# Relational layer of a graph network: loop product and bias made in the table stage, output stage written out

## The reference

```
W = (w_comp @ w_basis).reshape(8, 128, 128)      # one matrix per node type, from 4 bases
decomp(h) = einsum('ni,tio->tno', h, W)[node_type, arange(n)]
k, q, v = decomp_k(x), decomp_q(x), decomp_v(x)
kt = einsum('nhi,thij->tnhj', k, relation_att)[edge_type, src]     # vt likewise from v
e  = (q[dst] * kt).sum(-1) * relation_pri[edge_type] / 4
a  = softmax of e over the edges of each dst
agg = segment_sum(a * vt, dst)                   # sums divided by the softmax's sum
out = relu(decomp_a(agg) + x @ loop_weight + bias)
x = layernorm(x + out)
```

## Time and profile before

| | |
|---|---|
| median of 3 runs | 13184.11 us (13170.3 to 13192.89) |
| the profiled execution's own time | 13179.73 us |
| its span | 13177.8 us |
| PE, DVE, ACT, POOL busy | 52%, 50%, 16%, 53% of the span |
| mean granted clock of PE | 0.635 |

### The profile page before, as it was taken

How to read it: one execution, slowest core, us unless ns; L and a number is a source line. 1 busy time by engine, 2 the same in 40 slices (tenths; PEclk the granted TensorE clock), 3 DMA queues, 4 the chain that set the end, 5 groups by cost and what they waited for, 6 DMA issues and landing times. The chain is left out here.

```text
span 13177.8 us, 169349 instructions
## 1 busy us (share of the span) xinstructions
PE 6872.9 (52%) x37679; PEld 6012.4 (46%) x37680; DVE 6549.5 (50%) x22663; ACT 2082.2 (16%) x6208; POOL 7027.7 (53%) x7417
## 2 busy tenths in 40 slices
PE   5555444445554555100384555656666566665555
PEld 4444333335554555100234455456665465654444
DVE  6444455555555555200265555755556344455555
ACT  4222100001110111000121111311222111122222
POOL 6555566646664666777205555245553555535554
PEclk6555555556666666555687777877787555556766
DMA  0000011111111111010143222111112211112232
GB/s 19 1 1 1 21 44 44 44 42 42 42 43 40 42 42 43 16 22 8 50 157 79 74 74 74 56 38 39 39 39 65 52 38 38 38 47 77 79 81 74
DMA packets 436083, 614.60 MB, mean 47 GB/s; under 512 B 176625, under 2 KB 312133, under 8 KB 435173
## 3 DMA queue, kind: packets, MB, share of 16 engines
q0 software_dynamic: 257024, 486.93, 14.5%
q1 hardware_dynamic: 178369, 119.49, 3.2%
q10 hardware_dynamic: 292, 3.41, 0.1%
HBM read 520.17 MB, written 89.19 MB: 46 GB/s over the span
## 5 line engine op out<-in xcount | busy, mean ns | idle before, releaser
L1094 POOL DMA_INDIRECT hop_rows<-hops,k_src_gather x1568 | 1479.3, 943 | 1077.3 <-issue 435.9
L1137 PE MATMUL hop_sums<-hop_rows,hop_weighted 128*128 x4992 | 1159.9, 405 | 1110.7 <-DVE k_x L1184 736.1
L1137 PEld LDWEIGHTS hop_sums<-hop_rows,hop_weighted 128*128 128x128 f32 x4992 | 1009.7, 300 | 1201.7 <-issue 1200.4
L1443 POOL DMA_INDIRECT l_pass_rows<-related,k_dst_typed x832 | 786.2, 945 | 1216.8 <-POOLq L74 517.6
L1443 POOL DMA_INDIRECT l_pass_rows<-left_table,k_dst_other x832 | 786.6, 945 | 895.7 <-DVE l_pass_terms L1815 490.5
L1938 POOL DMA_INDIRECT l_weigh_rows<-row_table,l_weigh_ring x832 | 813.0, 977 | 733.8 <-ACT l_weigh_ring L1902 466.3
L1443 POOL DMA_INDIRECT l_pass_rows<-key_table,k_src_gather x784 | 739.5, 943 | 766.6 <-DVE l_pass_scores L1752 387.3
L726 POOL DMA_INDIRECT src_sorted<-src_scatter_records,src_scatter_places x784 | 750.6, 957 | 606.3 <-DVE src_scatter_places L714 393.6
L1538 PE MATMUL l_pass_sums<-l_pass_zero 128*128 128x272 bf16 (+1 forms) x1210 | 262.7, 306 | 1454.0 <-DVE l_total L1632 1005.2
L1094 POOL DMA_INDIRECT hop_rows<-in_x,k_src_gather x784 | 739.6, 943 | 456.4 <-issue 220.8
L1292 POOL DMA_INDIRECT dst_sorted<-rec,dst_places x784 | 809.2, 1032 | 262.1 <-issue 262.1
(11 more groups left out here) (467 smaller groups left out, 18342.8 us busy)
## 6 DMA issues: line engine op xcount, KB each, us to landing
related<-l_tables_rows SPq DMA_DIRECT2D x50, 1024.0 KB, 4.4
hop_rows<-hops,k_src_gather POOLq DMA_INDIRECT x1568
l_pass_rows<-related,k_dst_typed POOLq DMA_INDIRECT x832
l_pass_rows<-left_table,k_dst_other POOLq DMA_INDIRECT x832
l_weigh_rows<-row_table,l_weigh_ring POOLq DMA_INDIRECT x832
src_sorted<-src_scatter_records,src_scatter_places POOLq DMA_INDIRECT x784
hop_rows<-in_x,k_src_gather POOLq DMA_INDIRECT x784
dst_sorted<-rec,dst_places POOLq DMA_INDIRECT x784
```

Of the source, the lines that this page charges most:

```text
L1094: nc.gpsimd.indirect_dma_start(rows[:, s * G + g, :], None, table_in, bass.IndirectOffsetOnAxis(ap=o.gather[:, c:c + 1], axis=0),).then_in ...
L1137: last = nc.tensor.matmul(sums[:, b, g, :], weighted[:, s % SLOTS, g, :], rows[:, bass.ds(slots[g], 1), :], start=True, stop=True)
L1443: nc.gpsimd.indirect_dma_start(rows[:, s, g, :], None, table, bass.IndirectOffsetOnAxis(ap=index[:, c:c + 1], axis=0),).then_inc(got[s], 16)
```

## The change

In `relation_tables`, each step also makes `x @ loop_weight + bias` of its block: a 1-row product of ones with the bias and a 128x128 product accumulate in `turned[:, 1, :]`, ACT copies them to `looped`, and SP stores the block (64 KB) in `looped_home` in HBM. `relation_output` loads that array in five pieces instead of computing it, has no bias, no `inputs`, no `by`: POOL multiplies the sums by the inverses, PE turns them where they stand in `total`, the products have three buffers instead of two, DVE reads the type weights in `mix` and starts its chain from `looped`. The stage is written out for 25 pairs and has no loop. Removed lines of `relation_output` are left out below; they stand in the listing above.

```diff
-def relation_tables(nc, k, bases, att_sb, msg_sb, mix, queries, table, name, shared=None):
+def relation_tables(nc, k, bases, att_sb, msg_sb, mix, queries, table, loop_w, bias, looped_home, name, shared=None):
...
+            sp.dma_start(wl[:], loop_w).then_inc(loaded, 16)
+            sp.dma_start(bias_row[:], bias.rearrange("(a f) -> a f", a=1)).then_inc(loaded, 16)
             with sp.Fori(0, NBD // 2) as i:
                 for b in range(2):
                     n = i * 2 + b
+                    sp.wait_ge(looped_ok, n + 1)
+                    sp.dma_start(looped_home[:, bass.ds(n, 1), :], looped[:, b:b + 1, :]).then_inc(looped_stored[b], 16)
                     sp.wait_ge(left, n + 1)
                     sp.wait_ge(right, n + 1)
                     sp.dma_start(table[:, bass.ds(n * P, P), :].rearrange("t p f -> p t f"),
                                  rows[:, b, :, :]).then_inc(stored[b], 16)
             for b in range(2):
                 sp.wait_ge(stored[b], 16 * (NBD // 2))
+                sp.wait_ge(looped_stored[b], 16 * (NBD // 2))
...
+            def take_looped(n, b, saved):
+                act.wait_ge(turned_x, n + 4)
+                if saved is not None or at(n, 2):
+                    act.wait_ge(looped_stored[b], 16 if at(n, 2) else saved + 16 * (1 - b))
+                nc.scalar.copy(looped[:, b, :], turned[:, 1, :]).then_inc(looped_ok, 1)
...
             def step(n, b, saved):
                 if not at(n, NBD - 1):
                     own_rows(n + 1, 1 - b)
+                take_looped(n, b, saved)
+                if not at(n, NBD - 1):
                     take_turned(n + 1, 1 - b)
...
+            def loop_rows(b):
+                nc.tensor.matmul(turned[:, 1, :], one[:], bias_row[:], start=True, stop=False)
+                return nc.tensor.matmul(turned[:, 1, :], xt[:, b, :], wl[:], start=False, stop=True)
...
+                product = loop_rows(b)
                 if not at(n, NBD - 1):
                     turn_x(n + 1, 1 - b)
+                else:
+                    product.then_inc(turned_x, 1)
...
+                else:
+                    pe.wait_ge(looped_ok, NBD)
...
-            pe.wait_ge(loaded, 48)
+            pe.wait_ge(loaded, 80)
+            pe.wait_ge(one_ok, 1)
...
+def relation_output(nc, k, total, base, looped_home, mix, name):
...
+        looped = sb("looped", [P, NBD, D])
+        turned_sb = sb("turned_sb", [P, 2, 2, P])
...
+        based = ps("based", [P, 3, 2, BASES, D])
         loaded = sem("loaded")
+        looped_in = [sem(f"looped_in{p}") for p in range(PIECES)]
...
         def _(sp):
             sp.dma_start(w[:].rearrange("p (b o) -> p b o", b=BASES), base.rearrange("b (i o) -> i b o", o=D)).then_inc(loaded, 16)
...
+            for p in range(PIECES):
+                here = slice(p * PIECE, (p + 1) * PIECE)
+                sp.dma_start(looped[:, here, :], looped_home[:, here, :]).then_inc(looped_in[p], 16)
+        @block.gpsimd
+        def _(pool):
+            pool.wait_ge(step, 2)
+            for n in range(NBLK):
+                part = total[:, n, 0:D].rearrange("p (h f) -> p h f", h=HEADS1)
+                over = total[:, n, D:D + HEADS1].rearrange("p (h a) -> p h a", a=1).to_broadcast([P, HEADS1, D // HEADS1])
+                nc.gpsimd.tensor_tensor(part, part, over, ALU.mult).then_inc(
+                    normed, 1 if n < NBLK - 1 else 1 + NBD - NBLK)
...
         def _(act):
...
+            for n in range(pairs):
                 act.wait_ge(turned_ok, n + 1)
...
+                if n >= 2:
+                    act.wait_ge(based_ok, n - 1)
+                nc.scalar.copy(turned_sb[:, n % 2, :, :], turned[:, n % 2, 0:2, :]).then_inc(copied, 1)
...
         def _(pe):
...
+            def turn(n):
+                pe.wait_ge(normed, 2 * n + 2)
+                if n >= 2:
+                    pe.wait_ge(copied, n - 1)
+                for j in range(2):
+                    last = nc.tensor.transpose(turned[:, n % 2, j, :], total[:, 2 * n + j, 0:D], k.ident[:])
+                last.then_inc(turned_ok, 1)
+            pe.wait_ge(loaded, 16)
+            turn(0)
+            for n in range(pairs):
+                if n + 1 < pairs:
+                    turn(n + 1)
                 pe.wait_ge(copied, n + 1)
...
+                if n >= 3:
+                    pe.wait_ge(done, n - 2)
                 for j in range(2):
...
+                    last = nc.tensor.matmul(based[:, n % 3, j, :, :], turned_sb[:, n % 2, j, :], w[:], start=True, stop=True)
+                last.then_inc(based_ok, 1)
...
         @block.vector
         def _(dve):
             chain(nc.vector.tensor_single_scalar(den, den, TINY, ALU.max))
             chain(nc.vector.reciprocal(den, den))
...
+            made = [0]
+            def count(instruction):
+                made[0] += 1
+                instruction.then_inc(d, 1)
+            for n in range(pairs):
+                b = n % 2
+                if n % (PIECE // 2) == 0:
+                    dve.wait_ge(looped_in[n // (PIECE // 2)], 16)
+                dve.wait_ge(based_ok, n + 1)
                 for basis in range(BASES):
                     for j in range(2):
...
+                        if basis > 0:
+                            dve.wait_ge(d, made[0] - 1)
+                        elif n >= 2:
+                            dve.wait_ge(done, n - 1)
+                        own = looped[:, 2 * n + j, :] if basis == 0 else mixed[:, b, j, :]
+                        at_basis = mix[:, 2 * n + j, 3 * BASES + basis:3 * BASES + basis + 1]
+                        count(nc.vector.scalar_tensor_tensor(out=mixed[:, b, j, :], in0=based[:, n % 3, j, basis, :],
+                                                             scalar=at_basis, in1=own, op0=ALU.mult, op1=ALU.add))
+                dve.wait_ge(d, made[0])
+                here = k.x[:, 2 * n:2 * n + 2, :]
+                nc.vector.scalar_tensor_tensor(out=here, in0=mixed[:, b, :, :], scalar=0.0, in1=here, op0=ALU.max,
                                                op1=ALU.add).then_inc(done, 1)
...
```

More of the change, by code:

```diff
@@ L2338, in relation_tables @@
         w = sb("w", [P, 3, BASES * D])
+        wl = sb("wl", [P, D])
+        bias_row = sb("bias_row", [1, D])
+        one = sb("one", [1, P])
+        looped = sb("looped", [P, 2, D])
         x = sb("x", [P, 2, D])
@@ L2348, in relation_tables @@
         loaded = sem("loaded")
+        looped_ok = sem("looped_ok")
+        looped_stored = [sem("looped_stored0"), sem("looped_stored1")]
+        one_ok = sem("one_ok")
         own = sem("own")
@@ L2488, in step @@
                     take_rows(n - 1, 1 - b, saved)
+            nc.vector.memset(one[:], 1.0).then_inc(one_ok, 1)
             in_blocks(dve, step)
@@ L2753, in _ @@
                                             ALU.add).then_inc(normed_too, 1)
-def relation_output(nc, k, total, base, loop_w, bias, mix, name):
+def relation_output(nc, k, total, base, looped_home, mix, name):
     pairs = NBD // 2
@@ L2761, in relation_output @@
         w = sb("w", [P, BASES * D])
-        wl = sb("wl", [P, D])
-        bias_row = sb("bias_row", [P, D])
-        inputs = sb("inputs", [P, 2, 2, 2, D])
-        by = sb("by", [P, 2, 2, BASES])
-        turned_sb = sb("turned_sb", [P, 2, 4, P])
+        looped = sb("looped", [P, NBD, D])
+        turned_sb = sb("turned_sb", [P, 2, 2, P])
         mixed = sb("mixed", [P, 2, 2, D])
         turned = ps("turned", [P, 2, 4, P])
-        based = ps("based", [P, 2, 2, BASES, D])
-        looped = ps("looped", [P, 2, 512])
+        based = ps("based", [P, 3, 2, BASES, D])
         loaded = sem("loaded")
+        looped_in = [sem(f"looped_in{p}") for p in range(PIECES)]
+        step = sem("step")
         normed = sem("normed")
-        step = sem("step")
-        own = sem("own")
         turned_ok = sem("turned_ok")
@@ L2789, in _ @@
         @block.scalar
         def _(act):
-            def own_rows(n, b):
-                act.wait_ge(normed, n * 2 + 2)
+            for n in range(pairs):
                 act.wait_ge(turned_ok, n + 1)
-                nc.scalar.copy(inputs[:, b, 0, :, :], total[:, bass.ds(n * 2, 2), 0:D])
-                nc.scalar.copy(inputs[:, b, 1, :, :], k.x[:, bass.ds(n * 2, 2), :]).then_inc(own, 1)
-            def a_pair(n, b, last=False):
-                if not last:
-                    own_rows(n + 1, 1 - b)
-                act.wait_ge(turned_ok, n + 3)
-                act.wait_ge(based_ok, n + 1)
-                nc.scalar.copy(turned_sb[:, b, :, :], turned[:, b, :, :]).then_inc(copied, 1)
-                act.wait_ge(done, n + 1)
-                nc.scalar.copy(by[:, b, :, :], mix[:, bass.ds(n * 2, 2), 3 * BASES:4 * BASES]).then_inc(weights, 1)
@@ L2809, in _ @@
-            act.sem_inc(copied, 2)
-            own_rows(0, 0)
-            with act.Fori(0, pairs // 2) as i:
-                a_pair(i * 2, 0)
-                a_pair(i * 2 + 1, 1)
-            a_pair(pairs - 1, 0, True)
```

(26 more changed lines are left out.)

38 lines of the change are left out of this document (3 added, 35 removed).

## The result

Twenty runs of each kernel: 13209.58 us after, 13182.92 us before, ratio 1.0021 with a 95% interval of 1.0014 to 1.0027. That is 26.7 us slower (18 to 36), where 5.2 us were forecast: inside the range given, at its upper end, and on the border of the 0.2% that was called no change (the interval goes from 0.14% to 0.27%).

The account below looks back on a forecast made before the run. PE was taken to bound the table stage and DVE the output stage. +24.5 + 0.6 - 13.7 - 6.2 = +5.2 us on the profiled 13179.7 gave 13184.9; with 4.4 for the median, 13189 us, range 13172 to 13213.

Parts of the forecast that it names:

- The signs of being wrong: Stated failure limits: table step growing over 0.6 or under 0.4 us, pair over 2.9, or an untouched stage moving over 5.
- Nothing of the stage lies beside the scatter, PE's pace sets the step: Table stage: starts 132 us after the last DMA start of POOL's second scatter; always-busy PE sets its 6.34 us step.
- The one-row product costs 0.27, bounds 0.22 and 0.33: Table stage: price on PE per step of the added 1-row bias product, taken from 8-row products; 50 steps.
- Head of the tables +0.6: Start of the table stage: PE's first transpose waits for two more loads, 0.6 us later (bounds 0 and 1.0).
- Pair of 2.66 us, -13.7: Output stage: without DVE's first addition and the loop, 2.66 us per pair, 66.5 for 25 against 80.2, so -13.7 us.
- Head of the output stage -6.2: From the inverses to DVE's first pair: POOL multiplies at 0.45 us each, DVE starts at 8426.8 against 8432.98, -6.2 us.
- POOL and DVE get in each other's way: Output stage rival: some 45 POOL multiplications each hold a mixing operation, +13 to +27 us; net +25, 13209; chance 0.12.
- TensorE stays at 1.2 GHz: Output stage rival: PE at half clock needs 3.88 us per pair, more than DVE; net +35 us, 13219; chance 0.07.
- POOL far slower: Output stage rival: POOL over 1.33 us per operation sets the pair; at 2.0 us net +35, 13219; chance 0.07.
- a new wait in the tables: Table stage rival: ACT's extra copy or the stores cost 0.38 us per step; net +24, 13208; chance 0.06.
- products for nothing: Table stage rival: the two added products cost nothing as DVE sets the step; net -19, 13165; chance 0.05.
- main case: Whole kernel: the terms as summed, +5.2 us, with its own range of +1 to +11 us; chance 0.63.

## Why the prediction was right and where it was wrong

- *The signs of being wrong*: the step was not to grow by more than 0.6 us; it grew by 0.83, and the point on the one-row product says why. No untouched stage was to move by more than 5 us; several did (see the result), but kernels that are alike in a stretch do so too: from the tables' last transpose to the output stage four of them took 1646.7 to 1658.1 us on one chip. That sign was finer than one execution of each kernel can bear.
- *Nothing of the stage lies beside the scatter, PE's pace sets the step*: right in the executions it was made for. It is no property of the program, though: on another chip the stage lies beside the scatter.
- *A full product costs 0.22*: right (6.34 to 6.56).
- *The one-row product costs 0.27, bounds 0.22 and 0.33*: the step that failed. It is 0.61, 17 us over 50 steps more than forecast. The earlier trace rows showed two 8-row products side by side and the way back to 128 rows (0.33, against 0.41 here). The way in was left out: both bounds were taken behind the first small load, where it had been paid, and the 0.40 us of idle time ahead of that load went unread. That one time alone would not have given the price, as PE waited for DVE in it as well; but the trace before has 52 such loads in that pass, and they start 0.32 us (least and median) after the full load ahead of them, where full ones there are 0.11 apart. A way in of 0.2 us could be read from it.
- *Head of the tables +0.6*: +0.3. ACT's copy, SP's store and the waits for them cost nothing, as argued; the copy of 128 columns takes 0.27 us. The DMA share of the earlier trace rows is 0.49 and not 0.48; it fell to 0.46, as the steps are longer. Nothing hangs on it.
- *Pair of 2.66 us, -13.7*: the pair is 2.53, since with the loop the 0.16 us ahead of relu in the earlier trace rows went too. 25 pairs gave -16.9, of which the stall took 5.8 back; with 0.2 for the second relu, -10.9.
- *Head of the output stage -6.2*: -6.8, POOL's multiplication taking 0.40 us and starting each 0.36 (the estimate was 0.45).
- *POOL and DVE get in each other's way* (0.12, every mixing operation held): not so. No mixing operation was longer than 351 ns, beside POOL's multiplications or behind them, but one relu was held for some 17 of them. The sentence on the Trainium skill's rule had the right operation, and "a few times for part of a multiplication" was too small.
- *TensorE stays at 1.2 GHz*: no; 1.00 from 8470 on, though not from the second pair on as the signs had it. The 0.74 of the window before goes with PE's 4.64 idle us behind the stalled relu.
- *POOL far slower, a new wait in the tables, products for nothing*: none happened.

The sum was +5.2 and the places show +23.4: +16.3 from the table step, -0.3 from its head, and +2.2 from the output stage (stall +5.8, pairs -3.2, head -0.6, the second relu +0.2). The mechanism of the main case held; a unit price was less than half of the true one, and was paid 50 times.

## What to carry to other kernels

Don't put a product of fewer rows (1 and 64 were tried) between full-height ones on a TensorE that is never idle: fill its rows, group such products, or let an idle engine add the row. When POOL computes beside DVE, give each DVE operation that reads SBUF twice an input in PSUM, or let POOL wait so that the two don't coincide; whether a broken row would let such an operation through wasn't tried. And ask of any stage said to lie beside another whether the trace shows it on every chip, and whether work given to an engine would queue behind what that engine already has.

## What the hardware showed that was not expected

- A load of 1, or of 64, rows starts only when the stream of the full-height product before it is through (0.95 and 0.94 us behind the last load), a load of 128 rows does not wait for it (0.43); there and back costs 0.39 us. The Trainium skill, "TensorE: Matmul & The Clock Gate", section "The mechanism", says that a weight load overlaps products in flight only when its row group differs; here the load that covers all rows overlapped and the one that covers fewer did not, so for this form the measurement decides. The same section also lets a load into the background weight buffer run ahead; no run here shows which of the loads go there.
- POOL's multiplications start every 0.36 us while a record lasts 0.40, one running into the next. Relu ended 14.13 us after POOL's first multiplication in four traces (14.49 in two), though it had begun anywhere from 7.3 to 8.2 us after it; and at that point stands the one multiplication of 680 ns, 0.28 longer than the rest, which begins 0.42 us, a relu's length, before relu ends. So it looks as if relu got its turn only there. What opens the gap at that place of POOL's row was not tried.
- Why the polynomial's loads are slow beside the scatter on one chip and not on another stays open.
